# A second slot table from five groups, thirteen expert slots in the first phase, and GpSimd drains

## The reference, cut to what matters

```python
x = x + ga * _L0_attn_ref(h, ...)
h = _layernorm(x, axis=-1) * (1 + cb) + sb
gate_logits = jnp.einsum('bsd,ed->bse', h, gate_w) + gate_b + expert_bias
top_idx = jnp.argmax(gate_logits, axis=-1)
for e in range(NUM_EXPERTS):
    mask = (top_idx == e)[..., None].astype(x.dtype)
    h1 = jax.nn.relu(jnp.einsum('bsd,df->bsf', h, w1[e]) + b1[e])
    y = jnp.einsum('bsf,fd->bsd', h1, w2[e]) + b2[e]
    out = out + mask * y
x = x + gb * out
```

## Time and profile before

| | |
|---|---|
| time, median of 3 runs | 428.52 us (428.21 to 428.74) |
| the profiled execution, its time | 428.04 us |
| its span, first to last instruction | 426.3 us |
| mean granted clock of TensorE | 0.988 of full speed |
| PE busy | 384.9 us (90%) |
| weight loads (PEld) | 349.1 us (82%) |
| DVE, POOL, ACT busy | 347.0, 313.0, 297.0 us |
| DMA | 63.29 MB, mean 148 GB/s |

### The profile page before, as it was taken

One profiled execution on the slowest core, in us unless ns is written; L12 is line 12 of the kernel. 1 busy time (PEld: TensorE's weight loads), 2 busy tenths in 40 slices (PEclk: granted clock), 3 DMA queues, 4 the chain that ended last, 5 costly groups with the idle time before them and its releaser, 6 DMA issues. The chain is left out here.

```text
span 426.3 us, 10441 instructions
## 1 busy us (share of the span) xinstructions
PE 384.9 (90%) x3040; PEld 349.1 (82%) x3040; DVE 347.0 (81%) x1052; ACT 297.0 (70%) x854; POOL 313.0 (73%) x463
## 2 busy tenths in 40 slices
PE   8788989997998899698999889889999988999990
PEld 7657878897888798587889878879998977999990
DVE  6777789998879999989889997789697595788871
ACT  3776789797699988688687888898756633444430
POOL 4754894799995989679989889999956547645441
PEclk9999999999999999999999999999999999999996
DMA  8999999999920000001010110005821138888830
GB/s 239 325 334 335 334 336 332 334 335 333 312 94 2 1 2 2 0 15 37 2 52 2 50 52 1 2 2 175 312 89 50 62 106 232 263 234 216 233 102 0
DMA packets 54951, 63.29 MB, mean 148 GB/s; under 512 B 4604, under 2 KB 47996, under 8 KB 54768
## 3 DMA queue, kind: packets, MB, share of 16 engines
q1 hardware_dynamic: 50528, 55.76, 43.6%
q0 software_dynamic: 2784, 6.37, 4.2%
q10 hardware_dynamic: 1584, 0.50, 0.5%
HBM read 20.97 MB, written 42.09 MB: 148 GB/s over the span
## 5 line engine op out<-in xcount | busy, mean ns | idle before, releaser
L711 POOL TENSOR_TENSOR accb<-accb,prod 128x512 f32<-128x512 f32 x48 | 61.3, 1278 | 23.6 <-ACT accb L1082 19.6
L1975 DVE SCALAR_TENSOR_TENSOR bank<-raw,cw,bank 128x512 f32<-128x512 f32 x96 | 72.0, 750 | 2.9 <-ACT bank L1092 1.5
L744 POOL TENSOR_SCALAR lseg<-strict,av 128x128 f32<-128x128 f32 x128 | 47.8, 388 | 6.6 <-DVE av L1934 4.6
L989 POOL DMA_INDIRECT out_dram<-raw x30 | 29.2, 973 | 27.2 <-DVE raw L2420 22.7
L1515 PE MATMUL bank<-skip,cx 128*128 128x128 f32 x256 | 41.2, 283 | 7.4 <-DVE st L2023 7.0
L896 POOL DMA_INDIRECT routed_rows<-rows,rowat x32 | 32.2, 1006 | 15.7 <-issue 8.1
L1131 ACT ACTIVATE xt<-bank,dtv 128x128 f32<-128x128 f32 x128 | 39.5, 362 | 5.5 <-PE bank L1494 5.2
L1751 PE MATMUL bank<-raw 128*128 x312 | 43.3, 282 | 0.0
L1515 PEld LDWEIGHTS bank<-skip,cx 128*128 128x128 f32 x256 | 33.6, 191 | 10.3 <-DVE st L2023 9.5
L1531 PE MATMUL bank<-xt,ms 128*128 128x128 f32 x256 | 39.0, 275 | 0.0
L1508 PE MATMUL bank<-incl,lseg 128*128 128x128 f32 x256 | 38.9, 274 | 0.0
(11 more groups left out here) (273 smaller groups left out, 1141.3 us busy)
## 6 DMA issues: line engine op xcount, KB each, us to landing
routed_rows<-padrow SPq DMA_DIRECT2D x32, 1040.0 KB, 12.6
zs<-routed_rows SPq DMA_DIRECT2D x39, 130.0 KB, 3.4
xs<-in_w_dram SPq DMA_DIRECT2D x16, 258.0 KB, 3.5
hT<-in_w_dram SPq DMA_DIRECT2D x15, 258.0 KB, 3.4
zs<-in_w_dram SPq DMA_DIRECT2D x8, 258.0 KB
raw<-in_w_dram SPq DMA_DIRECT2D x1, 2048.0 KB, 10.1
xs<-in_u_dram SPq DMA_DIRECT2D x3, 512.0 KB, 8.6
routed_rows<-padrow SPq DMA_DIRECT2D x9, 130.0 KB, 3.9
```

The lines of the kernel that those rows point to most:

```text
L711: pool.tensor_tensor(accb[:, :], accb[:, :], prod[:, :], ALU.add).then_inc(s_tapb, 1)
L744: last = pool.tensor_scalar(lseg[:, Q % LA, h, :], strict[:, d, :], av[:, b, col(d, h, t)], 1.0, ALU.mult, ALU.mult)
L1975: dve.scalar_tensor_tensor(out=acc(S, g)[:, :], in0=raw[:, g, c0:c0 + BLK], scalar=cw[:, d, g, k:k + 1], in1=acc(S, g)[:, :], op0=ALU.mult ...
```

## The change

A second table is made on POOL from the counts of five groups (SECONDG), enough for KE = 13 slots; the four more (KS) are worked in the early phase. In detail:

- POOL: second_counts (ten small operations) behind numbers(7) and ahead of group 5's scatters; second_table (nine) behind these; taken_tiles (now four operations, of `taken`) from the last step to between the scatters of groups 6 and 7, and taken_first in its old place.
- SP: loads rows and weights of slots 9 to 12 when the second table is there and five groups have landed, ahead of the wait for the late table.
- PE and ACT: slots 9 to 12 in the early phase's manner. PE multiplies no ones at the join. The late phase has 26 slots.
- DVE: gdiff and the gates of six early slots ahead of choose(7); behind the table outputs 0 to 5, gates 6 to 12, outputs 6 to 9 and 10 to 12.
- POOL: a drain (`pool.drain()`) behind the last scatter, and one behind put(s) of each eighth late slot: slots 20, 28 and 36.

The diff, cut to its core:

```diff
-FIRSTG = 4
+FIRSTG, SECONDG = 4, 5
 K1 = -(-(FIRSTG * BLK - NE * (P - 1)) // P)
-assert 2 < K1 <= FIRSTG * BLK // P
+KE = -(-(SECONDG * BLK - NE * (P - 1)) // P)
+KS = KE - K1
+assert 2 < K1 < KE <= SECONDG * BLK // P and KS <= K1
...
+RETIRE = 8
...
-WARM_SCATTER, WARM_ROWS = 12, 6
...
+            sp_.wait_ge(s_firstv, 2)
+            landed(sp_, SECONDG)
+            for s in range(K1, KE):
+                at_row = first_row(s)
+                load_rows(s, at_row)
+                load_w1(s, at_row)
             sp_.wait_ge(s_tabv, 1)
-            first = [first_row(s) for s in range(K1, K1 + 2)]
+            first = [first_row(s) for s in range(KE, KE + 2)]
...
+            def second_counts():
+                hold(pool, s_rt_dve, NR * (SECONDG - 1) + 5)
+                link_first(pool.tensor_tensor(whole[:, :], nextrow[:, SECONDG % 2, :], region_mid[:, :], ALU.subtract))
+                assert nf[0] == NSECOND, nf[0]
+                link_first(pool.tensor_scalar(whole[:, :], whole[:, :], 1.0 / P, ROUND, ALU.mult, ALU.add))
+                link_first(pool.tensor_scalar(first, whole[:, :], ROUND, 1.0, ALU.subtract, ALU.mult))
+                pool.tensor_scalar(whole[:, :], first, -float(P), 0.0, ALU.mult, ALU.add)
+                for k, far in enumerate((1, 2, 4)):
+                    to = prefix[:, k + 1, NE // 2:] if k < 2 else sums2[:, :]
+                    link_first(pool.tensor_tensor(to, prefix[:, k, NE // 2:], prefix[:, k, NE // 2 - far:NE // 2 + NE - far],
+                                                  ALU.add))
+                link_first(pool.tensor_tensor(taken[:, :], sums2[:, :], used[:, :], ALU.subtract))
+                link_first(pool.tensor_scalar(taken[:, :], taken[:, :], float(KS), 1.0, ALU.min, ALU.mult))
+                link_first(pool.tensor_tensor(taken[:, :], taken[:, :], used[:, :], ALU.add))
+            def second_table():
+                wide = [P, KS, NE]
+                link_first(pool.tensor_tensor(coef1[:, :], coef1[:, :], whole[:, :], ALU.add))
+                link_first(pool.tensor_tensor(behind1[:, 1, 0:KS], behind1[:, 1, 0:KS],
+                                              sums2[:, :].unsqueeze(1).broadcast_to(wide), ALU.subtract))
+                link_first(pool.tensor_scalar(behind1[:, 1, 0:KS], behind1[:, 1, 0:KS], 0.0, 1.0, ALU.is_ge, ALU.mult))
+                link_first(pool.tensor_tensor(behind1[:, 0, 0:KS], behind1[:, 1, 0:KS],
+                                              coef1[:, :].unsqueeze(1).broadcast_to(wide), ALU.mult))
+                part_of, n = behind1[:, :, 0:KS, :], NE
+                for k in range(3):
+                    n //= 2
+                    to = summed[:, k, 0:2 * KS * n].rearrange("p (k s e) -> p k s e", k=2, e=n)
+                    link_first(pool.tensor_tensor(to, part_of[:, :, :, 0:n], part_of[:, :, :, n:2 * n], ALU.add))
+                    part_of = to
+                last = part_of.rearrange("p k s e -> p k (s e)")
+                link_first(pool.tensor_tensor(last[:, 0], last[:, 0], slot_at1[:, 0:KS], ALU.add))
+                pool.tensor_copy(slot_r1[:, :, K1:KE], last).then_inc(s_firstv, 1)
+            def taken_tiles():
+                differences(taken)
                 pool.tensor_scalar(coef, gain, float(P), float(REGION), ALU.mult, ALU.add).then_inc(s_over, 1)
                 pool.tensor_tensor(slot_of, slot_i[:, 0:K2].unsqueeze(2).broadcast_to([P, K2, NE]),
-                                   used[:, :].unsqueeze(1).broadcast_to([P, K2, NE]), ALU.add).then_inc(s_over, 1)
-                link_first(pool.tensor_scalar(slot_at, slot_i[:, 0:K2], used[:, 0:1], float(P), ALU.add, ALU.mult))
+                                   taken[:, :].unsqueeze(1).broadcast_to([P, K2, NE]), ALU.add).then_inc(s_over, 1)
+                link_first(pool.tensor_scalar(slot_at, slot_i[:, 0:K2], taken[:, 0:1], float(P), ALU.add, ALU.mult))
+                assert nf[0] == NFIRST, nf[0]
...
+                        taken_first()
...
+            second_counts()
             scatter(LASTG - 2, 0, 3)
             half_deviation(0)
             half_deviation(1)
             scatter(LASTG - 2, 3, BT)
+            second_table()
             scatter(LASTG - 1)
+            taken_tiles()
             scatter(LASTG)
-
-            for s in range(K1):
+            pool.drain()
+
+            for s in range(KE):
                 hold(pool, s_rb[s], 16)
-            pool.tensor_copy(tok1, rr[:, 0:K1, 2 * DM:2 * DM + 1]).then_inc(s_tok, K1)
+            pool.tensor_copy(tok1, rr[:, 0:KE, 2 * DM:2 * DM + 1]).then_inc(s_tok, KE)
...
             for s in range(NSLOT):
                 put(s)
-            hold(pool, s_put1, 16 * K1)
+                if s >= KE and (s - KE) % RETIRE == RETIRE - 1:
+                    pool.drain()
+            hold(pool, s_put1, 16 * KE)
...
-            for s in range(6, K1):
-                if s + 1 < K1:
+            for s in range(6, KE):
+                if s == K1 - 1:
+                    pe.wait_ge(s_firstv, 2)
+                if s + 1 < KE:
                     hidden(s + 1)
-                    if s + 2 < K1:
+                    if s + 2 < KE:
                         turn_rows(s + 2)
                 down(s, expert_of(s))
             pe.wait_ge(s_tabv, 1)
             for key in (("h2", LASTG, 0), ("h2", LASTG, 1), ("lg", LASTG), ("rk", LASTG)):
                 wait_free(pe, USE[key])
-            keep_warm(bank[high_low(K1 - 2)], WARM_SCATTER)
-            landed(pe, B * NBLK)
-            keep_warm(bank[high_low(K1 - 2)], WARM_ROWS)
-            turn_rows(K1)
-            turn_rows(K1 + 1)
-            hidden(K1)
-            for s in range(K1, NSLOT):
+            turn_rows(KE)
+            turn_rows(KE + 1)
+            hidden(KE)
+            for s in range(KE, NSLOT):
                 if s + 2 < NSLOT:
...
+            dve.wait_ge(s_tapb, HALO * NSTEP)
+            dve.tensor_tensor(gdiff, row[:, 1, 3, :], row[:, 0, 3, :], ALU.subtract).then_inc(s_gd, 1)
+            dve.wait_ge(s_gd, 1)
+
+            first_gates(0, 6)
             choose(LASTG)
             place(LASTG)
...
+            first_outputs(0, 6)
+            first_gates(6, KE)
+            first_outputs(6, 10)
+            first_outputs(10, KE)
+            rectify_high(KE)
+            for s in range(KE, NSLOT):
```

More of the change, by code:

```diff
@@ L533, in sum_bank @@
         def sum_bank(s):
[L534 removed]
+            return turn_bank(s + 1) if s < KE else bank[6 + s % 2]
         def high_low(s):
@@ L628, in _ @@
             for s in range(2):
-                load_rows(K1 + s, first[s])
-            for s in range(K1 + 2, NSLOT):
+                load_rows(KE + s, first[s])
+            for s in range(KE + 2, NSLOT):
                 at_row = first_row(s)
@@ L820, in first_table, with differences, taken_first @@
                 link_first(pool.tensor_tensor(last[:, 0], last[:, 0], slot_at1[:, :], ALU.add))
-                pool.tensor_copy(slot_r1[:, :, :], last).then_inc(s_firstv, 1)
-            def taken_tiles():
+                pool.tensor_copy(slot_r1[:, :, 0:K1], last).then_inc(s_firstv, 1)
+            def differences(of):
+                link_first(pool.tensor_tensor(gain[:, 0:NE - 1], of[:, 1:NE], of[:, 0:NE - 1], ALU.subtract))
+            def taken_first():
                 hold(pool, s_tab, NTAB0)
@@ L2320, in _, with link_early, first_gates, first_outputs @@
                         decay_copies(nxt)
+            ne = [0]
+            def link_early(ins):
+                ne[0] += 1
+                ins.then_inc(s_eo, 1)
+                dve.wait_ge(s_eo, ne[0])
+            def first_gates(s0, s1):
+                for s in range(s0, s1):
+                    dve.wait_ge(s_rb[s], 16)
+                link_early(dve.tensor_scalar(flag1[:, s0:s1], rr[:, s0:s1, 2 * DM:2 * DM + 1].rearrange("p s c -> p (s c)"),
+                                             float(L), None, ALU.is_ge))
+                for s in range(s0, s1):
+                    last = dve.scalar_tensor_tensor(out=gsel1[:, s, :], in0=gdiff, scalar=flag1[:, s:s + 1],
+                                                    in1=row[:, 0, 3, :], op0=ALU.mult, op1=ALU.add)
+                link_early(last)
+            def first_outputs(s0, s1):
+                dve.wait_ge(s_yo2, s1)
+                link_early(dve.tensor_tensor(ob1[:, s0:s1, :], ob1[:, s0:s1, :], gsel1[:, s0:s1, :], ALU.mult))
+                dve.tensor_tensor(ob1[:, s0:s1, :], ob1[:, s0:s1, :], rr[:, s0:s1, DM:2 * DM], ALU.add).then_inc(s_ob, s1 - s0)
             both(LASTG, 2, BT)
```

109 lines of the change are left out of this document (46 added, 63 removed).

## The result

The changed kernel took **425.85 us** (median of five runs, 424.92 to 427.41), the kernel before 428.52 in the same comparison: ratio 0.9939, 95% interval 0.9914 to 0.9964, so 2.7 us faster where 5.2 were forecast. Run once more in another comparison it stood at 0.9963 (0.9935 to 0.9991). The profiled execution took 425.85 us, its span is 424.1 for 426.3, its mean granted clock 0.979 for 0.988. The trace of after is 0.8 us later already in the last scan step, at the first of the two small operations of POOL on ssq for the last group (314.41, L765 of the kernel after, for 313.59, L754 of the kernel before).

What follows compares the result with a forecast made beforehand. PE sets the late pace at 2.007 us a slot, with a 6.8 us gap at the join and 5.9 us empty at the end; +3.1 -8.0 -1.3 +3.1 +1.6 +0.4 -4.1 = -5.2, so 423.3 us, range 420.5 to 427.0.

Steps and rivals of the forecast that it cites:

- The exit: Program end after the last landing: two indirect DMAs left to retire instead of 71, saving 4.1 us (0 to 5.7).
- Rival 1: Program end: drains wait for landings, but the exit keeps its 5.9 us; 424.5 us, chance 0.22.
- Group 7's scatters start 0.4 late: POOL before the join: after the inserted table pieces, these scatters start at 343.15 for 342.77.
- All this costs 0 to 0.4 us, hidden: POOL, SP and DVE before the join: the second table's work costs 0 to 0.4 us, hidden by the four slots.
- The early slots at 2.33 us: Early phase, slots 9 to 12: they run at ACT's pace, a loop of 2.33 us each.
- Hidden, by 0.7 us: SP's load of slot 13's rows behind the first drain: issued 353.1, landed 355.2 against 355.95 needed.
- The ring of four: Four out buffers: combine(17) waits for slot 13's store, held by the first drain; PE loses 3.1 us.
- DMA waits saved: PE's losses to late row loads, 0.95 early and 0.8 late: 1.3 us saved (0 to 1.8).
- I put no cost on the clock: PE at the join: idle time shrinks to some 0.5 us from 1.80 and 0.63, so no clock loss.
- Rival 2: POOL's drains: a drain does not wait, so stores are not held; 421.8 us, chance 0.13.
- rival 3: POOL's drains: each has a large price of its own and the exit stays; slower from 1.5 us each, chance 0.13.
- rival 4: Join: the second table comes late and PE stands before slot 9; 425.3 us at 2 us over, chance 0.07.

Runs made afterwards that it cites:

- a_same: The changed kernel run again unaltered, on the undisturbed chip: 426.49 us, ratio 0.9963 to the kernel before.
- b_drains_2: The kernel before plus drains behind the last scatter and each eighth late store, nothing else, on the undisturbed chip: 423.81 us, ratio 0.9878.
- b_drains: The kernel before plus drains behind the last scatter and each eighth late store, on a disturbed chip: 442.95 us, ratio 1.0070.
- a_no_drains_2: The changed kernel without all four drains, on the undisturbed chip: 424.14 us, ratio 0.9894 to the kernel before.
- a_no_first: The changed kernel without the drain behind the last scatter, the three late ones kept, on a disturbed chip: 440.55 us, ratio 0.9992.
- best: The changed kernel with drains only behind taken_first and slots 23 and 31, on a disturbed chip: 436.74 us, ratio 0.9929 to the kernel before.

## Why the prediction was right, and what was off in it

The time, 425.85, lies in the range, and the sign is right, because the two large terms were there: four late slots gone (-8.0) and most of the exit gone. The forecast's size was off by half, and that the sum did not come out further off is in part luck: a start of the late phase 3.6 us worse than forecast and 1.6 of half clock stand against 1.6 of exit, 0.8 of DMA waits, 0.5 at the last drain and 0.1 at the ring. (5.2 less these 2.2 is 3.0, and with the shift of 0.8 the span's 2.2.) Term by term:

- **The exit: mechanism right, size larger.** 69 DMAs fewer to retire gave 5.67 us, so 0.082 us for each, not the 0.06 taken, for which no row stood (it left 1.5 us for barriers); 1.6 us more than forecast. Six and seven left give 3.2 and 3.3 us (0.082 each on top of the 2.86 with two would give 3.2 and 3.3). Rival 1, the exit of fixed length, is refuted. The section of the Trainium skill that stood with it (Runtime: NRT & Kernel Launch, "The ~15µs preamble/postamble breakdown") lists one time for each part of the end; had they been all of it, the end would not have shrunk. The runs here do not show such a fixed part beyond what 2.86 us leaves behind the last landing.
- **The last drain: right in size.** 8.5 for 6.9 us from the last turn to the last store, +1.6 for the forecast's 1.6 and 0.4.
- **"Group 7's scatters start 0.4 late": this step failed.** It is 3.4 us. second_counts takes 3.7 us (324.43 to 328.18) for 2.9, since two of its 8-wide operations take 0.6 us where the nearest row gave 0.24; behind each inserted piece the next scatter starts 0.76 to 0.86 us later, not 0.3. So 4.6 us stand in the idle 2.24 before group 5's scatters, which start 2.6 us late (shift taken off) and not 0.9; second_table with its lag is 3.6 us (336.26 to 339.84) in the idle 2.89, and taken_tiles with its lag 2.1 (344.82 to 346.96) in the idle 2.52. POOL no longer waits for place, and the first delay goes through to the last scatter.
- **"All this costs 0 to 0.4 us, hidden": failed, by a path that the forecast left out.** Behind second_counts stand the two half_deviations as well, the norm of the last group. They start 2.6 us later too (332.75 for 329.33, less the shift), and PE's turn of that group's rows, which never waited before, waits for them: before and after, PE in order of time,

```profile
333.80 0.38 PE L1570 MATMUL bank<-ident,rows 128*128 128x128 f32 x2
```
```profile
335.46 0.41 PE L1636 MATMUL bank<-ident,rows 128*128 128x128 f32 x2 [0.52 <-DVE rows L2175]
```

  The products of slot 7 start at 342.51 for 340.62, 1.1 us late without the shift, ahead of any moved slot.
- **The early slots at 2.33 us: wrong, 2.50.** Between the turn and down PE loads the expert's number into a register (0.22 us idle, with no releaser), and products start as soon as down ends, so the loop is PE's own and not ACT's, as the forecast had it. The forecast took its pace from slots 7 and 8, which are the first pass of this loop. There the load has the same place, but from the turn to down only 0.21 us pass where later passes take 0.49, in the kernel before

```profile
341.59 0.27 PE L1612 MATMUL bank<-ident,zs 128*128 128x128 f32 x1
341.80 0.23 PE L1745 MATMUL bank<-b2p,b2one 96*128 x1
```

  and in the changed one (343.49 and 343.69) alike. Why the first pass is shorter is open. Over four slots this is 0.7 us.
- **"Hidden, by 0.7 us": failed with these.** With the scatters 3.4 us late and the drain 6.67 us for the 6.15 forecast (346.65 to 352.8), the row load of slot 13 was issued at 358.04, not 353.1, and PE waited 2.42 us. In sum the late phase started 6.7 us later where 3.1 was forecast. The run without drains shows the split: 5.1 without the drain (3.1 as forecast, 1.1 for the late norm, 0.7 for the pace, 0.2 beside them), 1.5 from the drain.
- **The ring of four: right in kind and size.** DVE waited 4.37 us before combine(17), PE 2.24; from 375.64 to 380.15 it lost 2.5 us where 3.1 was forecast. The drain behind slot 20, forecast as caught up, held DVE once more for 2.36 us at 395.20, and PE for 0.5. In a_same the first of these cost 4.9.
- **DMA waits saved: 1.3 forecast, 2.1 found.** In the trace of before the slots from the third late turn on lose 2.1 us against a pace of 2.01, all at or around waits for rows; in the changed kernel no late turn behind the second waits for rows.
- **"I put no cost on the clock": failed, 1.6 us.** It was put at nothing because the idle time at the join was to shrink to 0.5 us. PE stood idle 2.42 and 0.28 us there, and 3.4 us of half clock followed. From first to last late turn the changed kernel gained 5.6 us: 8.0 for four slots and 2.1 of DMA waits, less 3.0 at the ring and 1.6 of half clock.

Rival 2 (a drain does not wait) is refuted by 4.95 us of idle POOL, rival 3 (a price of its own) by the drain that cost nothing behind taken_first and by b_drains_2, 1.2% faster; rival 4 by PE, which never stood for the second table: it was written at 339.08, and the turn of slot 9 came at 345.70 without a wait.

The gain forecast and not found went to the start of the late phase and to the clock. In part this is interference: either half alone gives over 4 us on the undisturbed chip. Together the first drain stands ahead of a row load that the shorter gap has left with no slack, the stores it holds are now thirteen instead of nine, against a ring of four, and the clock falls behind PE's waits.

## What to carry to other kernels

A drain of POOL waits for landings and takes longer the more DMAs have not been retired, and the program's end pays a price for all that is left: so put drains where the engine is idle and the DMAs have long landed, and leave the last few for the exit. That a drain ahead of another queue's next load is the thing to avoid was argued from one wait of 2.42 us; moving the load's release ahead of the drain was tried on the disturbed chips, and was no faster than the kernel before (1.0055 and 1.0016). Three small pieces put into idle times of 2.2 to 2.9 us, each with a start lag behind it, filled them all, and then the delay of the first one went through to the last transfer: count a chain of such idle times once, not one by one, and follow everything else that stands behind the first piece. Price two edits together as well as alone when both spend the same gap. Where an edit leaves PE waiting, look at the granted clock behind the wait too: here it cost 1.6 and 2.4 us on top.

## What the runs showed that was not expected

- The end of the program shrinks with the number of indirect DMAs not yet retired by a drain: 8.53 us with 71, 3.3 with seven, 3.2 with six, 2.86 with two: 0.082 us each from the two ends. Nothing between seven and 71 was measured.
- From the last DMA's start to what follows a drain: 8.0 and 8.2 us with 53 to retire, 5.8 and 6.0 with 40, 4.3 to 6.7 with 32, 5.5 to 6.7 with 21, 5.0 and 5.6 with 17, and 3.3 to 5.8 with eight. So a drain is not simply one landing plus 0.082 us for each DMA. The clearest case against it is b_drains: SP's row load, which waits for all 32 scatters to land, is issued at 356.14, and the copy behind the drain starts at 357.07, 0.9 us later, where 32 at 0.082 would be 2.6. A drain may retire while it waits; that was not tried.
- An indirect DMA starts 0.76 to 0.87 us behind the small table operations and the copy of token numbers, 0.17 behind half_deviation (334.99), and 0.30 behind another indirect DMA. What makes the difference was not tried.
- 8-wide POOL operations take 0.20 us (L861) or 0.6 (L862 and L863, right behind it); L862 took 0.62 us in the traces of after, a_no_drains_2 and a_no_first, and 0.26 in that of best. Why was not tried.
- The granted clock of TensorE fell behind some idle times of PE and not behind others: not behind 2.23 us (a_same, 358.67) and 2.24 us (after, 379.61), but behind 2.42 and 0.28 in a row (after, 361.9) and within 4.21 us (a_same, 378.8). It stayed at 0.50 for 3.4 and 6.8 us, and cost 1.6 and 2.4 us there.
